# A gated cross-attention block on one core: rows behind the attention as one stream of 14 tiles, one ring of three lift buffers, maxima of two heads in one matmul

## What is computed

```python
def block(x, ctx_1024):                    # x (8, 224, 512), ctx_1024 (8, 750, 512)
    q = layer_norm(layernorm(x), gq, betq); c = layer_norm(ctx_1024, gkv, betkv)
    Q, K, V = q @ Wq + bq, c @ Wk + bk, c @ Wv + bv          # 16 heads of 32
    attn = softmax(Q @ K.T / sqrt(32))
    x = x + tanh(g_xattn) * (attn @ V @ Wo + bo)
    h = relu(layernorm(x) @ quantize(W1).T + b1)             # 2048 wide, weights in {-1, 0, 1}
    return x + tanh(g_ffn) * (h @ quantize(W2).T + b2)
```

## Time and profile before

| | us |
|---|---|
| median of three runs (970.43 to 975.07) | 974.21 |
| the profiled execution | 970.62 |
| its span, first to last instruction | 968.7 |

### The profile page before, as it was taken

How to read it: one execution, slowest core, us unless ns; L and a number is a source line. 1 busy time by engine, 2 the same in 40 slices (tenths; PEclk the granted TensorE clock), 3 DMA queues, 4 the chain that set the end, 5 groups by cost and what they waited for, 6 DMA issues and landing times.

```text
span 968.7 us, 22558 instructions
## 1 busy us (share of the span) xinstructions
PE 903.6 (93%) x8996; PEld 693.5 (72%) x8996; DVE 735.1 (76%) x1376; ACT 644.0 (66%) x1330; POOL 303.6 (31%) x519
## 2 busy tenths in 40 slices
PE   2897997889999999999999999999999999889768
PEld 0554665756888688867888688867888688668747
DVE  2667899888688887788688886788677767888521
ACT  1867678656787487657777587757877575678421
POOL 3140375354321343032421344043323223043023
PEclk9999999799999999999999999999999999999979
DMA  9489737550065003340146004440143006110000
GB/s 268 147 245 218 191 99 197 152 124 1 3 143 150 26 2 91 95 134 1 28 117 174 2 2 100 103 117 1 39 106 90 2 2 143 58 33 2 24 19 20
DMA packets 57104, 84.02 MB, mean 87 GB/s; under 512 B 6520, under 2 KB 33592, under 8 KB 57000
## 3 DMA queue, kind: packets, MB, share of 16 engines
q1 hardware_dynamic: 56568, 82.55, 32.5%
q10 hardware_dynamic: 432, 0.02, 0.0%
HBM read 42.20 MB, written 3.67 MB: 47 GB/s over the span
## 4 chain that ended last, share of the span: by engine, by line
PE 80%; DVE 8%; DMA 4%; SPq 3%; ACT 3%; issue 1%; POOL 0%; DVEq 0%; ACTq 0%; POOLq 0%
PE ps_fill L477 52%; PE ps_pv L524 8%; PE ps_score L492 8%; PE ps_exp L508 7%; PE ps_fill L534 4%; DVE row_max L785 2%; SPq L398 2%; DMA h_parts<-w2t 2%; PE ps_fill L583 2%; DVE p_parts L793 2%; DMA ctx_raw<-ctx_in 1%; DMA k_stack<-k_stage_lo 1%; SPq L407 1%; DVE ctx_t_lo L870 1%; DVE bn L825 1%
## 5 line engine op out<-in xcount | busy, mean ns | idle before, releaser
L793 DVE TENSOR_TENSOR p_parts<-ps_exp,p_parts 125x448 f16<-125x448 f32 x384 | 231.7, 618 | 61.8 <-ACT ps_exp L664 59.9
L785 DVE TENSOR_REDUCE row_max<-ps_score 128x1 f32<-128x750 f32 x256 | 239.0, 934 | 46.6 <-PE ps_score L492 45.8
L663 ACT ACTIVATE p_parts<-ps_exp 125x448 f16<-125x448 f32 x384 | 208.9, 544 | 95.2 <-PE ps_exp L508 81.1
L664 ACT ACTIVATE ps_exp<-ps_exp 125x448 f32<-125x448 f32 x384 | 211.0, 549 | 0.0
L492 PE MATMUL ps_score<-k_stack,q_stack 96*128 96x375 f16 x512 | 126.4, 328 | 12.7 <-DVE row_max L785 12.3
L508 PE MATMUL ps_exp<-q_stack,k_stack 99*125 99x224 f16 x768 | 128.1, 266 | 10.2 <-DVE p_parts L793 7.2
L524 PE MATMUL ps_pv<-v_now,p_parts 125*128 125x66 f16 x3072 | 116.1, 194 | 2.4 <-DVE p_parts L793 1.9
L524 PEld LDWEIGHTS ps_pv<-v_now,p_parts 125*128 125x128 f16 x3072 | 110.9, 98 | 8.4 <-DVE p_parts L793 2.1
L477 PE MATMUL ps_fill<-w_ternary,h_parts 128*128 128x256 fp8e4 x1024 | 116.6, 273 | 0.0
L508 PEld LDWEIGHTS ps_exp<-q_stack,k_stack 99*125 99x125 f16 x768 | 87.9, 137 | 34.6 <-DVE p_parts L793 10.1
L477 PEld LDWEIGHTS ps_fill<-w_ternary,h_parts 128*128 128x128 f16 x1024 | 99.7, 98 | 13.2 <-DVE ctx_t_lo L870 1.1
(11 more groups left out here) (139 smaller groups left out, 1549.0 us busy)
## 6 DMA issues: line engine op xcount, KB each, us to landing
k_stack<-k_stage_hi SPq DMA_DIRECT2D x64, 187.5 KB, 2.7
v_now<-v_stage SPq DMA_DIRECT2D x32, 346.5 KB
ctx_raw<-ctx_in SPq DMA_DIRECT2D x8, 1344.0 KB
h_parts<-w1t SPq DMA_DIRECT2D x16, 512.0 KB, 4.5
h_parts<-w2t SPq DMA_DIRECT2D x16, 512.0 KB, 5.0
k_stack<-k_stage_lo SPq DMA_DIRECT2D x32, 187.5 KB, 2.8
...
```

What stands on the lines that cost most here:

```text
L663: nc.scalar.activation(ph[0:KR, unit, :], ps_exp[0:KR, u, 0:2 * NQ], ACT.Exp, scale=EXP_SCALE)
L664: nc.scalar.activation(ps_exp[0:KR, u, 0:2 * NQ], ps_exp[0:KR, u, 0:2 * NQ], ACT.Exp, scale=EXP_SCALE).then_inc(exp_done, 1)
L785: nc.vector.tensor_reduce(mx[:, i // 2, i % 2:i % 2 + 1], ps_score[:, :, 0:KH], AX.XY, ALU.max) \
L793: nc.vector.tensor_tensor(pl[0:KR, unit, :], ps_exp[0:KR, u, 0:2 * NQ], ph[0:KR, unit, :], ALU.subtract).then_inc(p_split, 1)
```

## The change

- *Tiles.* Behind the attention the 8 x 224 rows are one stream of 14 tiles of 128 rows. `tiles_of(n)` gives 1 tile to batches 0 and 4 and 2 to each other; steps `op`, `op_add`, `norm2`, `yt`, `yt_lo`, `f2`, `f2_add` of a tile that isn't there are dropped from the list. `o_t` has two halves of 256 columns that alternate by batch; `o_pieces` splits an `ot` tile that crosses into the next batch's tiles in two pieces. f1 works on 128 or 256 columns. Residual and output are loaded and stored by whole tiles of the stream.
- *Lifts.* One ring `lifted` of three buffers in place of `qk_full` and `h_full`; a lift waits until GpSimd has subtracted the third lift before it, of whatever kind.
- *Maxima.* `mr` is two matmuls, one for each row tile, whose weights hold high and low part of both heads (4 columns); the result is copied to rows 96 to 99 of both heads, and the key rows hold -16 for the head's own two rows and 0 for the other's. The shift is folded into `split`. The selector is made on VectorE at the start.
- *Small things.* The reciprocal goes in place; several constants move into `h_parts`, which is free until f1 starts; `r1`, `r2` are one row shorter; partition p of the context holds rows 6p to 6p + 5, one run of 12 KB.
- *Order.* OPENING, ROUND and ENDING are written anew. In ROUND the steps of SP `kq.1` to `kq.3`, `vc`, `store` and `ctx` stand at the head, f2.2 follows f2.0 and f2.1 in the same round, and f2.3 opens the next.

The diff, without the order and the declarations:

```diff
+def tiles_before(n):
+    return n * NQ // P
+def tiles_of(n):
+    return tiles_before(n + 1) - tiles_before(n)
+def there(kind, i, n):
+    if kind in ("op", "op_add", "norm2", "yt", "yt_lo"):
+        return 0 <= n < B and i < tiles_of(n)
+    if kind in ("f2", "f2_add"):
+        return 0 <= n < B and i < 2 * tiles_of(n)
+    return 0 <= n < B
...
+LIFTS = [s for s in STEPS if s[0] in ("q", "k", "f1")]
+LIFT_AT = {s: k for k, s in enumerate(LIFTS)}
...
+        lifted = sb("lifted", [P, 3, 4 * P], F32)
+        o_t = [sb(f"o_t_{part}", [P, 2, DC, 2 * P], F16) for part in ("hi", "lo")]
...
+        PARTED = {"q": (qk_split, 10, 0), "k": (qk_split, 10, 2), "f1": (h_split, 8, 0)}
+        def parted(kind, i, n):
+            s, per_batch, first = PARTED[kind]
+            return s, n * per_batch + (first + i + 1)
...
+        def o_pieces(t, n):
+            at, end = n * NQ - tiles_before(n) * P, tiles_before(n + 1) * P - n * NQ
+            frm, to = q_cols(t)
+            cut = min(max(end, to.start), to.stop)
+            found = [(to.start, cut, n % 2, at), (cut, to.stop, (n + 1) % 2, -end)]
+            return [(slice(a - QSTART[t], b - QSTART[t]), half, slice(a + add, b + add))
+                    for a, b, half, add in found if b > a]
...
-                rows = ctx_in[n].rearrange("(i p) d -> p i d", p=KR)
+                rows = ctx_in[n].rearrange("(p i) d -> p i d", i=KT)
...
-                    for h in (2 * i, 2 * i + 1):
-                        for t in range(2):
-                            frm, to = q_cols(t)
-                            last = pe.matmul(
-                                ps_fill[SPLIT_ROWS:MAX_END, bank, (h % 2) * NQ + to.start:(h % 2) * NQ + to.stop],
-                                mhl[:, h, t, :], ident16[:, frm], start=True, stop=True,
-                                tile_position=(0, SPLIT_ROWS))
+                    for t in range(2):
+                        frm, to = q_cols(t)
+                        last = pe.matmul(ps_fill[SPLIT_ROWS:STACK_ROWS, bank, to], mhl[:, t, 2 * i:2 * i + 2, :],
+                                         ident16[:, frm], start=True, stop=True, tile_position=(0, SPLIT_ROWS))
...
+                    wide = tiles_of(n) * P
                     for j in range(2):
                         m = slice((2 * i + j) * P, (2 * i + j + 1) * P)
-                        last = three(ps_fill[:, bank, j * NQ:(j + 1) * NQ], lambda a, c: w1q[:, c, m],
-                                     lambda a, c: o_t[a][:, c, :], order=((0, 0), (0, 1)))
+                        last = three(ps_fill[:, bank, j * wide:(j + 1) * wide], lambda a, c: w1q[:, c, m],
+                                     lambda a, c: o_t[a][:, n % 2, c, 0:wide], order=((0, 0), (0, 1)))
...
+                if kind in ("q", "k", "f1"):
+                    lift = LIFT_AT[kind, i, n]
+                    if lift >= 3:
+                        act.wait_ge(*parted(*LIFTS[lift - 3]))
...
-                    if n:
-                        act.wait_ge(qk_split, n * 10 + (i - 1))
...
-                    act.wait_ge(qk_split, n * 10 + (i + 1))
...
-                    if i >= 2:
-                        act.wait_ge(h_split, n * 8 + (i - 1))
-                    elif n:
-                        act.wait_ge(h_split, n * 8)
...
-                nc.vector.reciprocal(rden[:, :, :], o_sum[:, :, :, HD]).then_inc(o_recip, 1)
+                nc.vector.reciprocal(o_sum[:, :, :, HD], o_sum[:, :, :, HD]).then_inc(o_recip, 1)
...
-                nc.gpsimd.tensor_scalar(mx[:, h2, :], mx[:, h2, :], 1.0 / M_SCALE, None, ALU.mult) \
+                nc.gpsimd.tensor_scalar(mx[:, h2, :], mx[:, h2, :], 1.0 / M_SCALE, -SHIFT, ALU.mult, ALU.add) \
```

More of the change, by code:

```diff
@@ L70 @@
-    v.0@1 k_hi.4@1 max.18@0 part.10@0 part.11@0 ternary.1@0 k_hi.5@1 max.19@0 take.2@0 split.3@0 score.22@0 pv.4@0
-    part.12@0 part.13@0 expo.18@0 expo.19@0 score.23@0 part.14@0 split.4@0 expo.20@0 max.20@0 v.1@1 mr.4@0 pv.5@0
-    expo.21@0 expo.22@0 ternary.2@0 expo.23@0 max.21@0 score.24@0 v.2@1 score.25@0 expo.24@0 part.15@0 take.3@0
-    vc.0@0 pv.6@0 part.16@0 part.17@0 rstd.0@2 max.22@0 expo.25@0 score.26@0 take.4@0 v.3@1 pv.7@0 score.27@0
-    ternary.3@0 ctx.0@2 part.18@0 v_lo.0@1 k_hi.6@1 part.19@0 max.23@0 load.14@0 part.20@0 expo.26@0 expo.27@0
@@ L110 @@
-    reload.15@0 ctx.0@3 vc.3@1 part.31@1 take.9@1 max.31@1 part.32@1 f1_hi.6@0 kq.0@2 part.33@1 cx_lo.0@3 split.7@1
-    max.0@2 f1_hi.7@0 expo.38@1 xx.0@3 f2.1@0 expo.39@1 cx.2@3 norm.7@3 norm.5@3 vc.0@2 score.3@2 vc.1@2 part.34@1
-    cx_lo.1@3 expo.40@1 part.35@1 cx.3@3 take.10@1 expo.41@1
+    bias_sum.0@0 norm.0@0 stat.6@0 w_hi.0@0 gain.0@0 norm.1@0 w_hi.1@0 load.0@0 stat.7@0 stat.0@0 stat.1@0 stat.2@0
+    stat.3@0 w_hi.2@0 norm.6@0 norm.7@0 w_hi.3@0 stat.4@0 stat.5@0 xx.0@0 xx.1@0 norm.2@0 w_hi.4@0 rstd.0@0
@@ new lines @@
+    w_lo.15@0 expo.4@0 expo.5@0 bo_add.0@0 xx_lo.1@1 q.1@1 piece_sum.13@0 split.0@0 part.0@0 piece_sum.14@0
+    score.11@0 piece_sum.15@0 k.0@1 max.9@0 load.10@0 expo.6@0 score.12@0 stat.0@2 part.1@0 k.1@1 part.2@0 stat.1@2
+    pv.0@0 max.10@0 split.1@0 q_hi.0@1 stat.2@2 shift_rows.0@0 score.13@0 expo.7@0 mr.2@0 kq.1@0 part.3@0 max.11@0
+    stat.3@2 part.4@0 stat.4@2 stat.5@2 expo.8@0 score.14@0 k.2@1 threshold.1@0 score.15@0 q_hi.1@1 max.12@0
+    expo.9@0 split.2@0 pv.1@0 k.3@1 part.5@0 max.13@0 load.11@0 k.4@1 score.16@0 take.0@0 stat.6@2 kq.2@0 max.14@0
@@ new lines @@
+    tot.1@0 kq.3@0 expo.10@0 k.5@1 score.17@0 part.6@0 expo.11@0 expo.12@0 k_hi.0@1 max.15@0 ctx.0@2 load.12@0 k.6@1
+    score.18@0 pv.2@0 k_hi.1@1 thr.1@0 stat.7@2 k_hi.2@1 part.7@0 k.7@1 expo.13@0 split.3@0 part.8@0 part.9@0
+    max.16@0 score.19@0 expo.14@0 pv.3@0 score.20@0 expo.15@0 mr.3@0 ternary.0@0 k_hi.3@1 part.10@0 max.17@0 v.0@1
+    take.1@0 expo.16@0 expo.17@0 score.21@0 k_hi.4@1 part.11@0 take.2@0 max.18@0 pv.4@0 expo.18@0 expo.19@0
+    ternary.1@0 norm.0@2 max.19@0 v.1@1 part.12@0 score.22@0 part.13@0 rstd.0@2 part.14@0 ternary.2@0 max.20@0
@@ new lines @@
+    max.1@1 part.37@0 cx.1@2 pv.11@0 score.2@1 pv.12@0 cx.2@2 cx_lo.0@2 take.11@0 part.38@0 load.13@0 load.14@0
+    load.15@0 vc.0@0 x.0@2 max.2@1 expo.39@0 ternary.11@0 score.3@1 score.4@1 max.3@1 norm.5@2 xx.1@2 cx_lo.1@2
+    expo.40@0 part.39@0 take.12@0 vc.1@0 reload.0@0 cx_lo.2@2 max.4@1 score.5@1 mr.7@0 cx.3@2 xx_lo.1@2 reload.1@0
+    reload.2@0 split.0@1 ternary.12@0 expo.41@0 expo.42@0 cx_lo.3@2 part.40@0 max.5@1 part.41@0 vc.2@0 q.0@2
+    part.42@0 expo.43@0 score.6@1 max.6@1 expo.44@0 pv.13@0 expo.45@0 take.13@0 ternary.13@0 score.7@1 part.43@0
@@ L113 @@
+    score.4@2 expo.41@1 cx.3@3 expo.42@1 ctx.0@3 pv.12@1 kq.0@2 score.5@2 cx.4@3 expo.43@1 max.1@2 f2_add.0@0
+    part.36@1 expo.44@1
 """
 ROUND = """
-    pv.12@-1 score.4@0 f2.2@-2 max.1@0 f2_add.0@-2 kq.1@0 part.36@-1 part.37@-1 take.11@-1 max.2@0 expo.42@-1 cx.4@1
-    xx_lo.0@1 score.5@0 part.38@-1 f2_add.1@-2 max.3@0 xx.1@1 pv.13@-1 cx_lo.2@1 part.39@-1 max.4@0 expo.43@-1
-    score.6@0 take.12@-1 cx_lo.3@1 expo.44@-1 f2.3@-2 score.7@0 part.40@-1 expo.45@-1 part.41@-1 mr.0@0 f2_add.2@-2
@@ new lines @@
+    part.38@-1 kq.2@0 xx_lo.0@1 f2.3@-2 kq.3@0 f2_add.1@-2 store.0@-2 ctx.0@2 max.3@0 part.39@-1 cx_lo.2@1
+    part.40@-1 max.4@0 vc.2@0 vc.3@0 part.41@-1 score.7@0 mr.0@0 expo.46@-1 cx_lo.3@1 f2_add.2@-2 take.12@-1 max.5@0
+    part.42@-1 cx_lo.4@1 expo.47@-1 part.43@-1 max.6@0 pv.14@-1 part.44@-1 take.13@-1 xx_lo.1@1 f2_add.3@-2 q.0@1
+    pv.15@-1 expo.0@0 cx.5@1 score.8@0 part.45@-1 max.7@0 part.46@-1 take.14@-1 part.47@-1 x.0@2 xb.0@-1 max.8@0
+    expo.1@0 q.1@1 score.9@0 take.15@-1 expo.2@0 k.0@1 cx_lo.5@1 divide.0@-1 part.0@0 q_hi.0@1 max.9@0 q_hi.1@1
```

454 lines of the change are left out of this document (234 added, 220 removed).

## The result

The change makes the kernel slower: 1000.75 us (median of six, 989.45 to 1004.57) against 972.39 (six, 969.7 to 975.07), a ratio of 1.024 with an interval of 1.020 to 1.028. The ratio is taken from fast runs alone, without the slowest of the six, and comes out lower than the 1.029 of the two medians: the loss is 24 to 28 us. The forecast of 948 (935 to 963) was wrong, and so was its sign. The removed work is gone as counted; the time went into gaps.

What follows compares the result with a forecast made beforehand. TensorE was taken to bound the five rounds. Gains of 17.3 us there, 9 before them and 1 at the start, less 2.4 at the end, took 970.6 to 945.7; an allowance for timed runs gave 948 us, range 935 to 963.

Steps and rivals of the forecast that it cites:

- What is removed: TensorE: 10.0 us per missing tile, all f1 together +0.6 us, mr 0.145 us less a step; about 8708 matmuls left.
- the rival of the small matmuls: TensorE: mr stays 0.29 us with two matmuls, or narrow f1 stays at 95.6 ns; 956 us, chance 0.09.
- In the rounds each PE nanosecond taken out is a nanosecond of the end, until VectorE fills: Five rounds, 288.3 to 825.3 us: removed TensorE time comes fully off the kernel's time; 17.3 us there.
- The freed time falls into stalls: Rival, rounds and 200 to 288 us: half of batch 4's 15.1 us and batch 0's 9 lost; 959 to 963, chance 0.15.
- my -2.4: 825.3 to 968.7 us: batch 7's longer f1 1.8 us, batch 6's f1 and mr -0.6; a loss of 2.4 us.
- Bounds for start and end together: 12 us either way: Start and end: the rewritten order moves the time by at most 12 us either way; 1 us gain taken.
- The moved steps in a round: SP's queue in the rounds: vc.2, the first needed, has 50 us of cover, so the new order causes no wait.
- The ring of three: Lifts sharing three buffers: waits for GpSimd were 7.8 us in the whole run; effect taken as 0.
- slower: the shared ring: Rival: lifts waiting on GpSimd hold back exps and starve TensorE; 984 us at 0.25 us a wait, chance 0.05.
- The context's longer runs: Start, batch 0's context load in 12 KB instead of 2 KB runs: at most 5 us shorter, 1 us taken.
- The sign: Whole kernel: chance 0.92 for faster, 0.03 for the same, 0.05 for slower.

Runs made afterwards that it cites:

- the old order: New tiles and two-head maxima in the step sequence of the kernel before, two lift rings, b2 not loaded: 972.73 us with 12 KB context runs, 972.60 with 2 KB.
- lighter maxima: VectorE's maxima over half of the score's columns: 955.33 us (0.985) with the tiles in the old order, 964.97 us (0.992) in the kernel before.
- later norms: Tiles and two-head maxima in the old order, 2 KB context runs, four of ScalarE's norm steps 10 to 25 steps later in ROUND: 969.04 us, ratio 0.997.
- the kernel with both repairs: Changed kernel with its opening in the old sequence up to the first f1 and five statistics per round 20 to 36 steps later: 972.00 us, ratio 1.001.
- the old opening: Changed kernel with its opening in the sequence of the kernel before up to the first f1, own rounds and ending: 983.04 us, ratio 1.011.

## Why the prediction was wrong, point by point

- **What is removed: right in count and nearly in price.** 8708 matmuls, as said. From the chain of the changed kernel, narrow f1 in batch 0, mr with two matmuls, wide f1:

```profile
281.46 0.89 PE ps_fill L519 x16
462.73 0.19 PE ps_fill L624 x2
...
484.89 1.75 PE ps_fill L519 x16
```

  56 ns a narrow matmul, as taken, and 109 a wide one. The Trainium skill (TensorE: Matmul & The Clock Gate, section "Wait — 56ns, not 53.3ns?") has both figures: some 62 ns with hardware decoding off, by which the narrow step would be 0.99, and 55.6 ns as measured for 128 columns; the trace agrees with the second, so the section doesn't speak against the term as the prediction had it. mr is 0.19, not 0.145: what it saves is 0.10 a step and not 0.145, 2.2 us less over the 48 steps that the sum counts. Two slips that moved nothing: 512 columns in 216 ns make 54 ns for 128 and not 53, and the rival of the small matmuls has 8 us of mr on the path where the sum has 7.0.
- **"In the rounds each PE nanosecond taken out is a nanosecond of the end, until VectorE fills": wrong, and this cost the forecast its 24 us.** The chain of a round shows what held the round as it was, not by how much. The others were close behind: half of f2 left out gave 3.7 of 7.0 us a round, at 83% of VectorE busy over the round and 92% in the stretch where f2 stands. Work that was added to TensorE (the wider f1) came in full, work that was removed came by half or not at all. "Until VectorE fills" was the right condition, taken from the wrong place: a mean share over the round for slack in the stretch that loses the matmuls. That the tiles' missing steps are lost in the same way is inferred from this run; in the old order it was not cut out by itself.
- **The freed time falls into stalls (0.15, 959 to 963).** The right mechanism with too small a price: half of batch 4's and all of batch 0's were to be lost (added to 948 that makes 965, not 959 to 963); in the old order 21.3 us were lost in three stretches and 5.4 more in opening and ending, all of the sum. The ending was 161.6 us for 158.7 by pitches; my -2.4 there should have been -5.8.
- **"Bounds for start and end together: 12 us either way": the failed bound that turned the sign.** The opening moved by 23.1 us. It was taken from the gaps that the start of before had, which bound what an order can win there, not what another order can lose. Two places of the diff could have been read for it: `bias_ready.0`, VectorE's wait for the bias rows' way through memory, stood 7 steps behind its `turn_bias.0` and 33 behind `cx_lo.0`; now it follows its DMA at once, ahead of `cx_lo.0`. And `stat.0` of batch 1 stands 3 steps behind the `cx_lo.5` that frees its buffer, for 28 before. The runs show that the order of the opening costs this; no run moves one of the two alone.
- **The moved steps in a round: "they would have to lose their cover to show one".** They had. I followed SP's queue (`vc.2`, 50 us of cover) and not VectorE's: `stat.0` stands 31 steps behind `cx_lo.5` in the new ROUND, where it stood 43 behind. In the trace of before the statistic came 12 us after the load's issue; in the changed kernel VectorE is there after 7, and a load takes 9. Moving five steps gave 7.6 and 11.0 us.
- **The ring of three: right, 0.** Measured 1000.66 for 1000.75. The rival "slower: the shared ring" named a wrong cause for a right sign. What I did not see is that the ring couples kinds so that the old order can't run at all, so that order and ring come as one.
- **The context's longer runs: 1 us expected, none found**, 972.0 for 972.6 in the kernel before. The Trainium skill's rule for larger transfers (Perfetto Trace Analysis, section "DMA Optimizations"), from 2 KB up, has all 5 us of the bound come; from 2 to 12 KB this kernel shows none of it.
- **The sign.** 0.92 for faster rested on a sum in which the order had no chance of its own to lose more than 12 us. Its loss against the kernel before is 28 us by the medians: 17.7 in the opening, 11.0 in the rounds; the tiles' 24 us of gain are the part that never appeared.

What stays open: of the 24 to 27 us that the tiles should have given in the old order, lighter maxima bring out 10.8 and later norms 3.6, each by itself. The rest I can't put on one engine. Lower clock in the gaps is in it (0.95 in one stretch of 108 us, where the kernel with both repairs had 1.00 and 3.4 us less), but it follows from gaps. Nor is it split which steps of the new opening cost the other 11 us between the first score and the first f1; the two context loads in the chain above stand there, and in the trace of the old opening one of them is left.
